# A shared expert begun inside the attention before it, value products one slot later, and gathers that add

## The chip, the cores and the metric

The kernel runs on one core of one Trainium2 chip. The metric is the time of one execution on the device in microseconds; the median of three runs of the kernel before is 1149.08 us (1148.59 to 1153.42). The engines have queues of their own and work in order: TensorE (PE, with its weight loads as PEld), VectorE (DVE), ScalarE (ACT), GpSimd (POOL) and SyncE (SP), which here only issues DMAs. They wait for one another on semaphores.

## The reference

All is in float32. x has 8 batches of 256 rows of 256 numbers. Eight layers follow one another, each added to x and each fed by the layer norm of x; the four attentions and experts among them are what the change touches:

```python
x = x + L0_xattn(norm(x), ctx, ...)     # attention 0: 16 heads, 77 context rows a batch, key mask, bias
x = x + L0_ffn(norm(x), ...)            # r * (relu(xk Wk)^2 Wv) with a token shift
x = x + L1_xattn(norm(x), ...)          # gelu MLP
x = x + L1_ffn(norm(x), ...)            # 8 experts, the best 2 for each row, width 352
x = x + L2_xattn(norm(x), ctx, ...)     # attention 2, causal mask
x = x + L2_ffn(norm(x), ...)            # shared expert, width 512, plus the best 1 of 8 experts
x = x + L3_xattn(norm(x), ctx, ...)     # attention 3
x = x + L3_ffn(norm(x), ...)            # int8 linear layer with one scale for all rows
```

`L2_ffn` is the shared expert `silu(x @ wg.T) * (x @ wu.T) @ wd.T` for all rows, and beside it for each row the expert with the largest logit of `x @ gate_w.T`, fed with the row times the logistic function of that logit.

## The kernel before

x stays in the core's memory (`X`, 16 tiles of 128 rows). The stages run one after another: setup, a0 (attention 0), f (both middle layers), e1 (the routed experts, 39 tiles of rows sorted by expert), a2 (attention 2), s2 (the shared expert, 16 tiles), e2 (its routed experts, 23 tiles), a3 (attention 3), q3. Each stage ends with `end_stage` (L334 to L337): PE, DVE, ACT and POOL drain, count up one semaphore, and wait until all four have.

An attention goes over 32 units, four to a batch. Its code is a loop over slots, written alike in the program of each engine; in a slot an engine does a step for several units at different stages of progress. The small functions at L255 to L291 say in which slot each step of batch b stands: the output projection in slot 4b + 7, the residual add in 4b + 8, the deviations of the next norm in 4b + 9, the transposes of its rows in 4b + 10, the logits of the router (a2 alone) in 4b + 11. For unit u, PE makes the scores in slot u (L1515), DVE adds the bias to them (L1020, L1024) and takes the maximum (L1028), POOL subtracts it (L584), ACT takes the exponential (L775), DVE sums and inverts (L1036, L1038), POOL or ACT copies the small parts (L569, L571 or L782, L784), PE transposes the probabilities (L1524 to L1526) in slot u + 2, ACT copies them out of PSUM (L798), and PE multiplies them with the values (L1538, L1541) in slot u + 3. Two units later DVE scales the product (L1047), PE projects a batch (L1447), DVE adds it to X (L955) and takes the statistics (L962, L967), POOL makes deviations and shifts (L518 to L529), ACT normalises (L734), and PE transposes the normalised rows (L1425).

In a2 and a3 the rows of the routed experts before must be put back into x first. POOL gathers them from DRAM with an indirect DMA (L549) into a buffer `YG`, two batches deep, and DVE adds them to X (`add_gathered`, L991 to L1006): in a2 with a gate for each row (L1002), in a3 plainly (L1005), two 128x256 adds a batch. Then come the statistics of the batch.

s2 is a `tile_pipeline` (L347 to L357): body s does one step for each of four successive tiles. On PE these are the gate and up products (L1731) of tile s - 1, the transposes of the product (L1741) of tile s - 2, and the down product (L1753) of tile s - 3. ACT copies the normalised transposed rows (L891), takes silu (L902), copies the transposes (L908); DVE multiplies (L1345) and adds to X (L1357). Beside that stands the routing for e2: DVE's `one_expert` (L1276), `tiles_of_experts` (L1287), `slots_of_rows` (L1303) in the first three bodies, PE's counts (L1700, L1701), and for each tile the normalised rows that DVE writes out (L1334) and POOL scatters to DRAM (L667). The weights of the down product come by a load that SP issues behind the border of a2 (L485, L487), and the last two experts' weights behind it (L491, L492).

Of the kernel before, what the change touches and what calls it, by code (L numbers as in the profile page):

```python
# [11 lines left out]
ALU = mybir.AluOpType  # L12
# [3 lines left out]
P = 128  # L16
B, S, D = 8, 256, 256
# [52 lines left out]
def build(nc, a):  # L70
    with ExitStack() as ctx:
# [58 lines left out]
        def carve(sizes, at=0):  # L130
            views = []
            for n in sizes:
# [75 lines left out]
        w_loaded = sem("w_loaded"); moe_loaded = sem("moe_loaded"); shared_loaded = sem("shared_loaded")  # L208
# [38 lines left out]
            ("setup", "a0", "f", "e1", "a2", "s2", "e2", "a3", "q3"))}  # L247
# [4 lines left out]
        LAYER = dict(a0=0, a2=1, a3=2)  # L252

# [46 lines left out]
        def slots_of(stage):  # L300

            return range(gather_slot(0, 0, 0, 1) if stage in FED_FROM else 0, transpose_slot(B - 1) + (2 if stage == "a2" else 1))
# [29 lines left out]
        FED = dict(a2=0, a3=B)  # L332
# [14 lines left out]
        def tile_pipeline(engine, body, tiles, depth):  # L347

            warm = -(-depth // 2) + 1
            for s in range(2 * warm):  # L350
                body((s, s % 2, s // 2), lambda lag, s=s: lag <= s)
# [43 lines left out]
        def _(sp):  # L395
# [116 lines left out]
        def _(pool):  # L512
# [27 lines left out]
            def gathers(stage, s):  # L540
# [3 lines left out]
                for b in range(B):  # L544
                    for t in range(T):
                        for k in range(K):
                            if gather_slot(b, t, k, K) == s:
                                after(pool, gathered_used, FED[stage] + b - 1 if b >= 2 else 0)
                                pool.indirect_dma_start(  # L549
                                    YG[stage][b % 2][:, t, k], None, BUFS[fed][1][:, :],  # L550
                                    bass.IndirectOffsetOnAxis(ap=slot_u[:, k, b * T + t:b * T + t + 1], axis=0)
                                ).then_inc(gathered[b % 2], 16)

            def attention(stage):
                layer, norms, order = LAYER[stage], NORM[stage], ORDER[stage]
                u0 = NU * layer
                for s in slots_of(stage):
# [18 lines left out]
                    bd = batch_at(deviations_slot, s)  # L576
# [8 lines left out]
                    bt = batch_at(transpose_slot, s)  # L585
# [1242 lines left out]
```

## Time and profile before

| what | us |
|---|---|
| median of three runs (lowest to highest) | 1149.08 (1148.59 to 1153.42) |
| the profiled execution | 1156.12 |
| its span | 1154.4 |
| PE busy | 917.6 (79%) |
| DVE busy | 570.6 (49%) |
| ACT busy | 445.6 (39%) |
| POOL busy | 382.6 (33%) |
| mean granted clock of PE, of full speed | 0.879 |

The shares are means over stages with different limits, so the profile is read by stretches: what each engine is busy with there, at which granted clock, and for what it waits. In a row of the timeline stand the start, the duration, the engine, the line of the kernel, the operation, what it writes and reads, how many instructions are taken together, and in brackets how long the engine was idle before and what ended that. Durations of matmuls overlap a little, so steps are taken from start to start.

### The profile page before, as it was taken

How to read it: one execution, taken by the hardware profiler on the slowest of the kernel's cores; microseconds unless marked ns; L12 is line 12 of the kernel's file. 1: busy time of each engine (PE TensorE's matmuls, PEld its weight loads, DVE VectorE, ACT ScalarE, POOL GpSimd, SP SyncE). 2: the span in 40 equal slices, each digit the busy share in tenths (PEclk: the TensorE clock that was granted, in tenths of full speed). 3: DMA queues.
4: the chain of work that ended last, by engine and by line, in shares of the span. 5: the costliest groups of instructions: out<-in, count | busy, mean ns of one | idle time of the engine just before them, and what ended most of it. 6: DMA issues, size and time to landing. Idle time of an engine off the chain costs nothing. (4 is left out here: it accounts for less than half of the span.)

```text
span 1154.4 us, 18959 instructions
## 1 busy us (share of the span) xinstructions
PE 917.6 (79%) x5718; PEld 625.3 (54%) x5719; DVE 570.6 (49%) x1298; ACT 445.6 (39%) x874; POOL 382.6 (33%) x725
## 2 busy tenths in 40 slices
PE   6688865887699999916767759996999996867773
PEld 5455544776466666614445535663666664545541
DVE  4688854675621222238776724221111135687764
ACT  4355534653132222215544532221222224546544
POOL 5556632355300000056664511110000024566540
PEclk9799987998599999957887969998999996888885
DMA  5599003011221111139000012002111110000002
GB/s 173 181 373 384 29 1 114 10 47 42 85 71 59 59 57 59 53 75 360 29 28 10 2 36 110 23 24 68 43 44 45 41 44 19 14 11 15 2 1 74
DMA packets 72861, 84.17 MB, mean 73 GB/s; under 512 B 8299, under 2 KB 64595, under 8 KB 72787
## 3 DMA queue, kind: packets, MB, share of 16 engines
q1 hardware_dynamic: 68179, 70.65, 18.5%
q0 software_dynamic: 4608, 12.59, 3.3%
q8 instruction: 40, 0.66, 0.2%
q14 instruction: 34, 0.28, 0.1%
HBM read 45.73 MB, written 37.49 MB: 72 GB/s over the span
## 5 line engine op out<-in xcount | busy, mean ns | idle before, releaser
L1731 PE MATMUL PS<-WE,tmp 128*128 x496 | 186.5, 520 | 0.0
L1345 DVE TENSOR_TENSOR tmp<-PS,tmp 128x352 f32<-128x352 f32 (+1 forms) x78 | 47.4, 608 | 270.9 <-ACT tmp L902 270.7
L584 POOL TENSOR_TENSOR tmp<-tmp,small 128x616 f32<-128x616 f32 x96 | 116.6, 1215 | 114.5 <-DVE small L1028 113.9
L798 ACT ACTIVATE tmp<-PS 128x768 f32<-128x768 f32 x96 | 78.0, 812 | 140.2 <-PE PS L1526 139.7
L902 ACT ACTIVATE tmp<-PS 128x352 f32<-128x352 f32 (+1 forms) x78 | 41.5, 532 | 221.4 <-PE PS L1731 221.4
L1731 PEld LDWEIGHTS PS<-WE,tmp 128*128 128x128 f32 x496 | 91.6, 195 | 60.2 <-issue 35.8
L1753 PE MATMUL PS<-WE,tmp 128*128 (+1 forms) x418 | 101.0, 380 | 2.1 <-DVE tmp L1361 2.1
L1524 PE MATMUL PS<-ident,tmp 128*128 128x128 f32 x384 | 70.3, 313 | 39.2 <-POOL rsx L571 24.8
L549 POOL DMA_INDIRECT WE<-ys,slot_u x32 | 32.2, 1005 | 196.6 <-DMA ys<-tmp 187.9
L1425 PE MATMUL PS<-ident,XN 128*128 128x128 f32 x208 | 40.8, 329 | 62.2 <-ACT XN L734 61.9
L734 ACT ACTIVATE XN<-X,SHIFTS,RSTDS 128x256 f32<-128x256 f32 x104 | 56.6, 594 | 83.3 <-POOL SHIFTS L529 83.2
L1524 PEld LDWEIGHTS PS<-ident,tmp 128*128 128x128 f32 x384 | 50.5, 159 | 58.9 <-POOL rsx L571 34.0
L1028 DVE TENSOR_REDUCE small<-tmp 128x8 f32<-128x616 f32 x96 | 76.3, 795 | 8.9
L1753 PEld LDWEIGHTS PS<-WE,tmp 128*128 128x128 f32 (+1 forms) x418 | 74.6, 190 | 10.9 <-issue 3.3
L1036 DVE TENSOR_REDUCE small<-tmp 128x8 f32<-128x616 f32 x96 | 75.0, 782 | 4.4 <-issue 3.2
L1538 PE MATMUL PS<-tmp,VL 32*32 32x128 f32 x768 | 43.5, 299 | 40.4 <-ACT tmp L798 35.8
L775 ACT ACTIVATE tmp<-tmp 128x616 f32<-128x616 f32 x96 | 68.5, 713 | 17.3 <-POOL tmp L584 16.8
L1425 PEld LDWEIGHTS PS<-ident,XN 128*128 128x128 f32 x208 | 27.2, 165 | 78.0 <-issue 59.8
L1447 PE MATMUL PS<-W,tmp 128*128 128x256 f32 x256 | 67.2, 409 | 1.6 <-ACT XT L741 1.6
L1731 PE MATMUL PS<-W,tmp 128*128 128x512 f32 x128 | 60.0, 613 | 4.4 <-DMA tmp<-in_L_sdT 4.4
L894 ACT ACTIVATE tmp<-PS 128x256 f32<-128x256 f32 x62 | 23.9, 385 | 89.4 <-PE PS L1719 89.4
L1024 DVE TENSOR_TENSOR tmp<-PS,tmp 128x616 f32<-128x616 f32 x64 | 50.2, 784 | 16.3 <-PE PS L1515 16.0
(251 smaller groups left out, 1678.9 us busy)
## 6 DMA issues: line engine op xcount, KB each, us to landing
xs_regions<-WE SPq DMA_DIRECT2D x11, 1536.0 KB, 13.7
ys<-tmp SPq DMA_DIRECT2D x62, 128.0 KB, 1.7
WE<-in_L_w SPq DMA_DIRECT2D x16, 352.0 KB
tmp<-xs_regions SPq DMA_DIRECT2D x39, 128.0 KB, 2.0
WE<-in_L_rgT SPq DMA_DIRECT2D x8, 512.0 KB
WE<-in_L_ruT SPq DMA_DIRECT2D x8, 512.0 KB
WE<-in_L_rdT SPq DMA_DIRECT2D x8, 512.0 KB
tmp<-xs SPq DMA_DIRECT2D x23, 128.0 KB, 2.0
```

The lines of the kernel that those rows point to most:

```text
L584: pool.tensor_tensor(sc, sc, spread(mx[:, q], SK), ALU.add).then_inc(shifted, 1)
L734: last = act.activation(dst[:, t], X[:, row], ACT.Identity, scale=RSTDS[:, row:row + 1], bias=SHIFTS[:, row:row + 1])
L775: act.activation(SC[:, k % 4], SC[:, k % 4], ACT.Exp, scale=FAR if stage == "a3" else 1.0).then_inc(exp_done, 1)
L798: act.activation(PT[:, u % 4], PT_PSUM, ACT.Copy).then_inc(pt_ready, 1)
L1024: dve.tensor_tensor(sc.rearrange("p (c h k) -> p c h k", c=CHUNKS, k=SK), S_PSUM.rearrange("p c (h k) -> p c h k", k=SK), bias, ALU.add).t ...
L1028: dve.tensor_reduce(mx[:, k % 2], sc.rearrange("p (h k) -> p h k", h=HG), AX.X, ALU.max, negate=True).then_inc(max_ready, 1)
L1036: dve.tensor_reduce(sm[:, q], SC[:, k % 4].rearrange("p (h k) -> p h k", k=SK), AX.X, ALU.add)
L1425: last = pe.transpose(PS[:, BANK_X, g * S + t * P:g * S + (t + 1) * P], src[:, t, g * P:(g + 1) * P], ident[:, :])
L1447: last = pe.matmul(PS[:, bank, t * D:(t + 1) * D], left[:, c, t * P:(t + 1) * P], right[:, c], start=c == 0, stop=c == G - 1)
L1524: pe.transpose(PT_PSUM[:, c * P:(c + 1) * P], p[:, c * PAIR:c * PAIR + P], ident[:, :])
L1731: last = pe.matmul(PS[:, 2 * q + k, 0:F], XS[:, q, c], w, start=c == 0, stop=c == G - 1)
L1753: last = pe.matmul(PS[:, 6, 0:D], HT[0:n, q, c], w, start=c == 0, stop=c == chunks - 1)
```

## The change

Three things change.

- There is no border between a2 and s2. The first four bodies of the shared expert's pipeline stand in the last slots of a2, on PE, ACT and DVE, and the pipeline goes on from body 4. On PE the gates of tile 0 stand behind the last transposes of probabilities, those of tile 1 with the transposes of tile 0 behind the last output projection, those of tile 2 with the transposes of tile 1 and the down product of tile 0 behind the last transposes of rows. The routing moves: `one_expert` to the end of a2, the counts and `tiles_of_experts` to body 4, `slots_of_rows` and the first four rows out to body 5. Since tiles 0 and 1 have by then been added to X, POOL keeps a copy of their rows, from which the first two rows out are made. SP's load of the down weights waits for the last output projection, with a semaphore of its own.
- In a0 the value products and all that follows them stand one slot later (`LATE`).
- In a3 the indirect DMA adds the gathered rows to X itself; DVE's adds, the buffer and the wait for its release are gone.

The diff, cut to its core:

```diff
-        YG = dict(a2=(WE[:, (E - 1) * EW:(E - 1) * EW + 2 * T * D], QTf[:, 0:2 * T * D]),
-                  a3=(WE[:, EW:EW + T * D], WE[:, EW + T * D:EW + 2 * T * D]))
-        YG = {stage: [f.rearrange("p (t k d) -> p t k d", t=T, d=D) for f in pair] for stage, pair in YG.items()}
+        YG = [f.rearrange("p (t k d) -> p t k d", t=T, d=D)
+              for f in (WE[:, (E - 1) * EW:(E - 1) * EW + 2 * T * D], QTf[:, 0:2 * T * D])]
...
+        LATE = dict(a0=1, a2=0, a3=0)
...
+        def first_tile(body, s):
+
+            body((s, s % 2, s // 2), lambda lag: lag <= s)
+
+        def tile_pipeline(engine, body, tiles, depth, begun=0):
+
+            warm = 3 if begun else -(-depth // 2) + 1
+            for s in range(begun, 2 * warm):
+                first_tile(body, s)
...
-            sp.wait_ge(stage_done, 4 * ST["a2"])
-
+            sp.wait_ge(o_psum, SUM["a2"] + B)
             sp.dma_start(shared_wd.rearrange("p (c d) -> p c d", c=4),
-                         a["L2_sdT"].rearrange("(c p) d -> p c d", p=P)).then_inc(shared_loaded, 16)
+                         a["L2_sdT"].rearrange("(c p) d -> p c d", p=P)).then_inc(down_loaded, 16)
...
-                                after(pool, gathered_used, FED[stage] + b - 1 if b >= 2 else 0)
-                                pool.indirect_dma_start(
-                                    YG[stage][b % 2][:, t, k], None, BUFS[fed][1][:, :],
-                                    bass.IndirectOffsetOnAxis(ap=slot_u[:, k, b * T + t:b * T + t + 1], axis=0)
-                                ).then_inc(gathered[b % 2], 16)
+                                rows_of = bass.IndirectOffsetOnAxis(ap=slot_u[:, k, b * T + t:b * T + t + 1], axis=0)
+                                if stage == "a3":
+                                    pool.indirect_dma_start(X[:, b * T + t], None, BUFS[fed][1][:, :], rows_of,
+                                                            compute_op=ALU.add).then_inc(gathered[b % 2], 16)
+                                    continue
+                                after(pool, gathered_used, b - 1 if b >= 2 else 0)
+                                pool.indirect_dma_start(YG[b % 2][:, t, k], None, BUFS[fed][1][:, :],
+                                                        rows_of).then_inc(gathered[b % 2], 16)
...
-                    bd = batch_at(deviations_slot, s)
+                    bd = batch_at(deviations_slot, s - LATE[stage])
...
-            end_stage(pool, "a2")
+            pool.wait_ge(ot_ready, NU)
+            pool.tensor_copy(XD[:, 2:4], X[:, 0:2]).then_inc(raw_kept, 1)
...
+                    if stage == "a2" and s == NU:
+                        act.wait_ge(s_taken, u0 + NU)
+                        first_tile(shared_tile, 0)
+                    if stage == "a2" and s in (NU + 2, NU + 5, NU + 6):
+                        first_tile(shared_tile, {NU + 2: 1, NU + 5: 2, NU + 6: 3}[s])
+
+                if stage != "a2":
+                    end_stage(act, stage)
...
+                if stage == "a3":
+                    return
                 for k in range(K):
                     if k:
                         dve.drain()
                     for t in range(T):
-                        x, y = X[:, b * T + t], YG[stage][b % 2][:, t, k]
-                        if stage == "a2":
-                            last = dve.scalar_tensor_tensor(out=x, in0=y, scalar=gate[:, k, b * T + t:b * T + t + 1], in1=x,
-                                                            op0=ALU.mult, op1=ALU.add)
-                        else:
-                            last = dve.tensor_tensor(x, x, y, ALU.add)
+                        x = X[:, b * T + t]
+                        last = dve.scalar_tensor_tensor(out=x, in0=YG[b % 2][:, t, k],
+                                                        scalar=gate[:, k, b * T + t:b * T + t + 1], in1=x,
+                                                        op0=ALU.mult, op1=ALU.add)
                 last.then_inc(gathered_used, 1)
...
-                    if s % 2 == 0 and 4 <= s <= NU + 2:
-                        scaled_outputs((s - 4) // 2)
+                    if bl is not None and stage == "a2" and s < NU:
+                        logits_copied_from(bl)
+                    if (s - LATE[stage]) % 2 == 0 and 4 <= s - LATE[stage] <= NU + 2:
+                        scaled_outputs((s - LATE[stage] - 4) // 2)
...
+                    if stage == "a2" and s == NU + 3:
+                        first_tile(shared_tile, 1)
+                    if stage == "a2" and s == NU + 4:
+                        logits_copied_from(B - 2)
+                        first_tile(shared_tile, 2)
+                    if stage == "a2" and s == NU + 7:
+                        first_tile(shared_tile, 3)
+                        logits_copied_from(B - 1)
+                        one_expert()
+                dve.drain()
+                if stage != "a2":
+                    end_stage(dve, stage)
...
-                    if stage == "s2" and isinstance(i[0], int) and i[0] < 3:
-                        (one_expert, tiles_of_experts, slots_of_rows)[i[0]]()
-                    if stage == "s2" and live(2):
+                    if stage == "s2" and isinstance(i[0], int):
+                        if i[0] == 4:
+                            tiles_of_experts()
+                        if i[0] == 5:
+                            slots_of_rows()
+                            for t in range(2):
+                                rows_out_of_x(t, 2 + t, 0, XD[:, 2 + t])
+                            for t in (2, 3):
+                                rows_out_of_x(t, t % 2, 0)
+                        if i[0] == 3:
+                            dve.wait_ge(raw_kept, 1)
+                    if stage == "s2" and (not isinstance(i[0], int) or i[0] >= 6) and live(2):
                         rows_out_of_x(i[0] - 2, i[1], (i[2] - 1) * 16)
...
+                    if 0 <= s - 3 - LATE[stage] < NU:
+                        values(s - 3 - LATE[stage])
...
-                    bo = batch_at(out_proj_slot, s)
+                    bo = batch_at(out_proj_slot, s - LATE[stage])
...
+                    if stage == "a2" and s == NU + 1:
+                        pe.wait_ge(s_taken, u0 + NU)
+                        pe.wait_ge(shared_loaded, 16 * 2)
+                        first_tile(shared_tile, 1)
+                    if stage == "a2" and s == NU + 3:
+                        pe.wait_ge(pt_ready, u0 + NU)
+                        first_tile(shared_tile, 2)
+                        next_logits(B - 2)
+                    if stage == "a2" and s == NU + 6:
+                        pe.wait_ge(down_loaded, 16)
+                        first_tile(shared_tile, 3)
+
+                if stage != "a2":
+                    end_stage(pe, stage)
```

PE's row at the end of a2, before: from the last value products on (L1538, L1541; L1425 transposes rows, L1491 makes logits, L1447 is the output projection, L1731 the gates of a tile, L1700 and L1701 the counts, L1741 its transposes).

```order
L1538 MATMUL PS<-tmp,VL 32x128 x4
L1541 MATMUL PS<-tmp,WE 32x128 x4
L1425 MATMUL PS<-ident,XN 128x128 x4
L1491 MATMUL PS<-WR,XT 128x8 x4
L1447 MATMUL PS<-WE,tmp 128x256 x4
L1425 MATMUL PS<-ident,XN 128x128 x4
L1491 MATMUL PS<-WR,XT 128x8 x4
L1731 MATMUL PS<-W,tmp 128x512 x4
L1700 MATMUL PS<-tmp 128x128
L1701 MATMUL PS<-tmp 128x128
L1731 MATMUL PS<-W,tmp 128x512 x4
L1741 MATMUL PS<-ident,tmp 128x128 x4
```

The same stretch of PE after the change, from the gates of tile 0 on (L1792 gates, L1802 transposes of a tile, L1814 down product; L1586 and L1589 value products, L1473 rows, L1495 output projection, L1539 logits).

```order
L1792 MATMUL PS<-W,tmp 128x512 x4
L1586 MATMUL PS<-tmp,VL 32x128 x4
L1589 MATMUL PS<-tmp,WE 32x128 x4
L1473 MATMUL PS<-ident,XN 128x128 x4
L1495 MATMUL PS<-WE,tmp 128x256 x4
L1792 MATMUL PS<-W,tmp 128x512 x4
L1802 MATMUL PS<-ident,tmp 128x128 x4
L1539 MATMUL PS<-WR,XT 128x8 x4
L1473 MATMUL PS<-ident,XN 128x128 x4
L1792 MATMUL PS<-W,tmp 128x512 x4
L1802 MATMUL PS<-ident,tmp 128x128 x4
L1814 MATMUL PS<-tmp 128x256 x4
```

Three gates, two transposes of tiles and one down product now stand among the attention's last steps, ahead of the last logits; the counts have moved behind the gates of tile 3.

DVE's row in a steady batch of a3, before, with what it waits for (L1005 adds the gathered rows, L962 and L967 are the statistics).

```order
L1020 SCALAR_TENSOR_TENSOR tmp<-PS,tmp 128x616 [waits s_copied,s_psum]
L1028 TENSOR_REDUCE small<-tmp 128x8 [waits shifted]
L1005 TENSOR_TENSOR X<-X,WE 128x256 [waits gathered0]
L1005 TENSOR_TENSOR X<-X,WE 128x256
L962 BN_STATS st<-X 128x6 x2
L967 BN_AGGR mv<-st 128x2 [waits veps_ready]
L967 BN_AGGR mv<-st 128x2
L1036 TENSOR_REDUCE small<-tmp 128x8 [waits exp_done]
```

The same place after the change (L980 and L985 are the statistics, L1046 the maximum, L1065 the scaled outputs, L1101 the maximum for q3).

```order
L1038 SCALAR_TENSOR_TENSOR tmp<-PS,tmp 128x616 [waits s_copied,pt_psum,s_psum]
L1046 TENSOR_REDUCE small<-tmp 128x8 [waits shifted]
L1065 TENSOR_TENSOR tmp<-PS,tmp 128x256 [waits pv_done]
L980 BN_STATS st<-X 128x6 [waits gathered0]
L980 BN_STATS st<-X 128x6
L985 BN_AGGR mv<-st 128x2 [waits veps_ready]
L985 BN_AGGR mv<-st 128x2
L1101 TENSOR_REDUCE amax<-XN 128x1 [waits xn_ready]
L1054 TENSOR_REDUCE small<-tmp 128x8 [waits pt_psum,exp_done]
```

The two adds are gone; the wait for the gather is now on the first of the statistics.

## Rows read from the trace of the kernel before

**Rows 1.** Windows: stretch; its length and PE, PEld, DVE, ACT, POOL busy; clock; DMA.
```profile
650.00:670.00 20.00, 13.44 (x159) 8.82 (x157) 13.85 (x30) 10.99 (x24) 8.87 (x15) 0.99 0.00 1
669.15:697.18 28.03, 15.79 (x55) 10.10 (x55) 4.44 (x16) 6.32 (x11) 2.04 (x8) 0.51 0.28 102
697.18:708.02 10.84, 10.84 (x40) 6.17 (x38) 7.67 (x37) 3.69 (x8) 0.00 (x0) 1.00 0.22 77
700.00:780.00 80.00, 80.00 (x286) 48.51 (x286) 25.72 (x74) 20.27 (x43) 13.52 (x14) 1.00 0.07 23
50.00:150.00 100.00, 83.51 (x941) 56.46 (x941) 81.03 (x154) 53.12 (x84) 61.81 (x120) 0.97 0.73 255
```

**Rows 2.** Timeline of PE at the border of attention 2 and the shared expert.
```profile
668.88 0.27 PE L1526 MATMUL PS<-ident,rsx 128*128 128x128 f32 x1
...
675.32 3.75 PE L1447 MATMUL PS<-WE,tmp 128*128 128x256 f32 x8 [0.36 <-DVE LG L1064]
...
684.11 1.09 PE L1425 MATMUL PS<-ident,XN 128*128 128x128 f32 x4 [5.03 <-ACT XN L734]
...
692.21 6.05 PE L1731 MATMUL PS<-W,tmp 128*128 128x512 f32 x8 [4.39 <-DMA tmp<-in_L_sdT]
...
702.42 3.60 PE L1731 MATMUL PS<-W,tmp 128*128 128x512 f32 x8
705.85 0.60 PE L1741 MATMUL PS<-ident,tmp 128*128 128x128 f32 x4
706.29 1.89 PE L1753 MATMUL PS<-tmp 128*128 128x256 f32 x8
708.02 3.60 PE L1731 MATMUL PS<-W,tmp 128*128 128x512 f32 x8
```

**Rows 3.** Timeline of DVE, and of SP's queue, at the same border.
```profile
679.18 0.69 DVE L955 TENSOR_TENSOR X<-X,PS 128x512 f32<-128x512 f32 x1 [4.01 <-PE PS L1447]
...
703.71 0.16 DVE L1305 COPY tmp<-tmp 128x8 f32<-128x8 f32 x1
...
707.57 0.41 DVE L1334 TENSOR_SCALAR tmp<-X,MEANS,RSTDS 128x256 f32<-128x256 f32 x1
...
707.89 0.69 DVE L1345 TENSOR_TENSOR tmp<-PS,tmp 128x512 f32<-128x512 f32 x1
...
708.99 0.42 DVE L1357 TENSOR_TENSOR X<-X,PS 128x256 f32<-128x256 f32 x1
...
688.16 0.37 SPq L487 DMA_DIRECT2D tmp<-in_L_sdT  x1
```

**Rows 4.** Timeline of PE, then of DVE, in a batch of attention 0.
```profile
95.40 0.54 PE L1515 MATMUL PS<-KBD,tmp 32*128 32x154 f32 x8
96.38 0.42 PE L1538 MATMUL PS<-tmp,VL 32*32 32x128 f32 x8 [0.43 <-ACT tmp L798]
...
109.91 0.54 PE L1515 MATMUL PS<-KBD,tmp 32*128 32x154 f32 x8
...
99.18 0.69 DVE L955 TENSOR_TENSOR X<-X,PS 128x512 f32<-128x512 f32 x1 [1.48 <-PE PS L1447]
```

**Rows 5.** Attention 3: line L1005, a batch's timeline (DVE, POOL, PE), line L549.
```profile
L1005 DVE TENSOR_TENSOR X<-X,WE x16: 412/1154/1495, 945.6 to 1072.2; 128x256 f32<-128x256 f32 x16
...
1030.22 2.57 DVE L1005 TENSOR_TENSOR X<-X,WE 128x256 f32<-128x256 f32 x2
...
1031.06 1.45 POOL L588 TENSOR_TENSOR X<-X,rows 128x512 f32<-128x512 f32 x1
...
1034.12 0.18 POOL L518 COPY MEANS<-mv 128x2 f32<-128x2 f32 x1 [1.61 <-DVE mv L967]
...
1036.18 0.66 PE L1524 MATMUL PS<-ident,tmp 128*128 128x128 f32 x4 [3.21 <-POOL rsx L571]
...
L549 POOL DMA_INDIRECT WE<-ys,slot_u x16: 944/1035/1039, 937.7 to 1059.0; - x16
...
DMA to landing us min/median/max: 2.7/2.8/3.1
```

More of the change, by code:

```diff
@@ L300, in slots_of @@
         def slots_of(stage):
-            return range(gather_slot(0, 0, 0, 1) if stage in FED_FROM else 0, transpose_slot(B - 1) + (2 if stage == "a2" else 1))
+            return range(gather_slot(0, 0, 0, 1) if stage in FED_FROM else 0, transpose_slot(B - 1) + LATE[stage] + (2 if stage == "a2" else 1))
         def norm_order(stage):
@@ L790, in attention @@
                         xt_evacuate_at(norms + order["in", bi], bi)
[L791 removed]
+                    bt = batch_at(transpose_slot, s - LATE[stage])
                     if bt is not None:
@@ L877, in _, with expert_tile @@
             end_stage(act, "f")
-            def experts(stage):
+            def expert_tile(stage):
                 F, u0 = WIDTH[stage], FIRST[stage]
@@ L894, in body @@
                             act.activation(XS[:, q], PS[:, 7, 0:D].rearrange("p (g s) -> p g s", g=G), ACT.Copy).then_inc(xs_ready, 1)
-                    if stage == "s2" and isinstance(i[0], int) and i[0] == 1:
-                        act.wait_ge(route_dve, 1)
-                        act.activation(score[:, :], top[:, 0], ACT.Tanh, scale=0.5).then_inc(route_act, 1)
                     if live(1):
@@ L912, in body, with experts @@
                         last.then_inc(ht_ready, 1)
-                tile_pipeline(act, body, NT if stage == "s2" else SLOTS[stage], 2)
+                    if stage == "s2" and isinstance(i[0], int) and i[0] == 4:
+                        act.wait_ge(route_dve, 1)
+                        act.activation(score[:, :], top[:, 0], ACT.Tanh, scale=0.5).then_inc(route_act, 1)
+                return body
+            def experts(stage, body, begun=0):
+                tile_pipeline(act, body, NT if stage == "s2" else SLOTS[stage], 2, begun)
                 end_stage(act, stage)
-            experts("e1")
+            shared_tile = expert_tile("s2")
+            experts("e1", expert_tile("e1"))
             attention("a2")
-            experts("s2")
-            experts("e2")
+            experts("s2", shared_tile, 4)
+            experts("e2", expert_tile("e2"))
             keys_evacuate(G, False)
@@ L1362, in body, with experts @@
                             dve.drain().then_inc(y_ready, 1)
-                tile_pipeline(dve, body, NT if stage == "s2" else SLOTS[stage], 3)
+                return body
+            def experts(stage, body, begun=0):
+                tile_pipeline(dve, body, NT if stage == "s2" else SLOTS[stage], 3, begun)
                 end_stage(dve, stage)
+            shared_tile = expert_tile("s2")
             slots_of_results()
@@ L1565, in attention @@
                     bl = batch_at(logits_slot, s)
-                    if bl is not None and stage == "a2":
+                    if bl is not None and stage == "a2" and s != NU + 3:
                         next_logits(bl)
@@ L1574, in attention @@
                         queries(bq)
-                    bo = batch_at(out_proj_slot, s)
+                    bo = batch_at(out_proj_slot, s - LATE[stage])
                     if bo is not None:
                         out_projection(bo)
-                    for slot_of, which in ((in_transpose_slot, "in"), (transpose_slot, "out")):
-                        bt = batch_at(slot_of, s)
+                    for slot_of, which, late in ((in_transpose_slot, "in", 0), (transpose_slot, "out", LATE[stage])):
+                        bt = batch_at(slot_of, s - late)
                         if bt is not None and (which, bt) in order:
@@ L1732, in body @@
                         last.then_inc(h_psum, 1)
-                    if stage == "s2" and isinstance(i[0], int) and i[0] == 1:
+                    if stage == "s2" and isinstance(i[0], int) and i[0] == 4:
                         counts()
@@ L1754, in body, with experts @@
                         last.then_inc(y_psum, 1)
-                if stage == "s2":
-                    pe.wait_ge(shared_loaded, 16 * 3)
-                else:
+                return body
+            def experts(stage, body, begun=0):
+                if stage != "s2":
                     pe.wait_ge(moe_loaded, MOE_LOADED[stage])
-                tile_pipeline(pe, body, NT if stage == "s2" else SLOTS[stage], 3)
+                tile_pipeline(pe, body, NT if stage == "s2" else SLOTS[stage], 3, begun)
                 end_stage(pe, stage)
+            shared_tile = expert_tile("s2")
             pe.wait_ge(blocks_ready, 8)
-            experts("e1")
+            experts("e1", expert_tile("e1"))
             pe.wait_ge(w_loaded, 16 * 7)
             attention("a2")
-            experts("s2")
-            experts("e2")
+            experts("s2", shared_tile, 4)
+            experts("e2", expert_tile("e2"))
             pe.wait_ge(w_loaded, 16 * 11)
```

47 lines of the change are left out of this document (18 added, 29 removed).

## Prediction

> **What bounds the kernel now.** The windows by stretch come first, since every stage has another limit. In attention 0 no engine is full: in the hundred microseconds from 50 PE works 83.51 and DVE 81.03 [rows 1]. In the shared expert PE has no gap, 80.00 of 80.00 at full clock [rows 1]; nothing beside it costs time there unless it stops PE. Between them lies the end of attention 2: from 669.15, the end of the last transposes, to 697.18 PE works 15.79 of 28.03 us, with a granted clock of 0.51, which is the lower level, 1.2 GHz, nearly throughout; before it the clock was 0.99 [rows 1]. Then the timeline of PE at that border: the output projection of the last batch takes 3.75 us, the normalised rows are waited for 5.03, and after the last logits the first gate matmuls start at 692.21 behind 4.39 us of waiting for the shared down weights, whose load is issued only at 688.16, past the border [rows 2, 3]. They run at the lower level for 6.05 us; the next take 3.60 [rows 2]. Last, the waits of a steady batch in attentions 0 and 3, below.
>
> **The border.** What the change removes is a stretch of PE. Both kernels do the same work between the end of the last transposes and the gates of tile 3 (708.02 before): 38.87 us. In units of the full clock the work in it is 15.79 x 0.51 + 10.84 = 18.9 [rows 1]. After the change PE has a tile's gates to do whenever it waited: gates 0 cover the wait for the last copied probabilities, gates 1, transposes and a batch's logits the 5.03 us for the normalised rows (3.43 + 0.44 us and the logits), gates 2 the copy behind them. The down weights are asked for when the last projection is done (679.07 before, about 678 after); they took 692.21 - 688.16 = 4.05, so they are there at 682.5, and gates 2, which wait for them, come at about 685: hidden with 2 us to spare.
>
> The clock falls before gates 0 have begun to count, so I charge them their measured 6.05 against 3.60: 2.45; and 1 us for waits of under half a microsecond that stay. 18.9 + 2.45 + 1 = 22.3, against 38.87: 16.5 saved [rows 1, 2]. One cost comes back: route work that stood beside the slow first gates now stands in bodies 4 to 6. Body 5 of DVE holds the slot numbers (703.71 to 707.57, 3.86), four rows out at 0.41, a product at 0.69 and an add at 0.42: 6.6 us against a tile of PE of 5.6: gates 3.43, transposes 0.44, down 1.73, from start to start between 702.42 and 708.02 [rows 2, 3]. The difference and some waits, 1.0 to 1.5 us, show once as a PE wait for the output buffer to be read. **Border: -15.** Bounds: if the clock stays low until gates 3, the 18.9 become 38, and hardly 1 us is saved; if the low clock and the route work cost nothing, 38.87 - 18.9 - 1 = 19. I take -15 since dense gates brought the clock back at 697.18, five microseconds after their start [rows 1, 2].
> The copy of the raw rows on POOL and the early table load of ACT lie in stretches in which those engines waited; POOL worked 2.04 us of the 28.03 [rows 1]. The six expert loads go out about 10 us sooner behind the shared load, off the path.
>
> **Attention 0, values one slot later.** Scores of two successive batches start at 95.40 and 109.91: 14.5 us a batch. In each of four slots PE waits 0.43 for the copied probabilities before its value product, and DVE waits 1.48 once a batch for the output projection before the residual add [rows 4]. One slot later both are there. Then DVE needs 14.5 - 1.48 = 13.0 and PE 14.5 - 4 x 0.43 = 12.8: DVE is the bound. Ends: nothing (if the loop turns on POOL's shift and DVE's maximum), and 7 x 1.48 = -10.4. New: queries stand one slot behind the projection and wait for its buffer to be read, a few tenths. I take 13.35 a batch, nearest the DVE figure: seven intervals of 1.15, **-8**. The tail has one slot more, but its value products were waiting there for the copies, so it costs nothing.
>
> **Attention 3, adding gathers.** DVE's pair of adds takes 2.57 in a steady batch; one alone took 0.41 at the least and 1.15 at the median [rows 5]. Behind it come the statistics, then POOL's deviations (1034.12, after a wait of 1.61 for DVE), then the copies that PE waits 3.21 for [rows 5]. When the adds go, the statistics are ready before POOL has finished its bias add (1031.06 + 1.45 = 1032.5), so that is late next: POOL starts at 1032.5 instead of 1034.12, 1.6 a batch. Six batches have the pair on the chain; of two of them I take 1.5, between twice 0.41 and 2.57: 4 x 1.6 + 2 x 1.5 = 9.4. The first batches, before POOL is busy, give 2 x 0.41 = 0.8: -10. Against it stands the issue on POOL. A gather's issue takes 1.04 there, and two stand in each batch just ahead of the copies that PE waits for [rows 5]. What an adding one takes no row shows. Below: as long as the plain one, and if it was issued without its wait a little less: -11. Above: if it doubles, 13 issues on the chain by 1.04 cost 13, so the stage loses 3. I take a quarter of a microsecond more each, near the row: -10 + 3, **-7**. Landing (2.7 to 3.1) is covered by some 15 us between issue and use; only at the stage's start is it open, once [rows 5].
> The trace shows only the issue of plain gathers, at 1.04. The Trainium skill, in "Collectives: The Full Stack", section "The bandwidth ceiling: the fold count and why AG ≠ RS ≠ AR", says that an add on the way needs two source reads and so two read descriptors a chunk where a copy needs one. If POOL's time goes by descriptors, the sum would be rival C's 1129; by the row alone the gathers cost 3 less than I take, 1116. No run here shows it yet.
>
> **Sum.** -15 - 8 - 7 = -30 on the profiled execution's own 1156.12 (its span is 1154.4): 1126.1. That execution is 7 us above the median of the runs, 1149.08; in proportion, 1149.08 x 1126.1 / 1156.12 = 1119.
>
> **Rivals.** A: the clock does not come back in the tail, because short transposes and waits lie between the gates. For it: from 669.15 to 697.18 it stayed low through 3.75 us of projection [rows 1, 2]. Against: those stood beside idle times of 5.03 and 4.39. If it comes back only with the end of gates 1, two gates (6.9), the projection (half of 3.75) and some 1.3 of values and transposes run at the low level and lose their own 10.1 again, of which 2.45 are charged: 7.6 more, border -8, total -23, 1126. [...]
> B: attention 0 turns on DVE-POOL-ACT hand-overs, not on the waits that go; PE and DVE both had about a fifth idle [rows 1]. Then 0 there: -22, 1127.
> C: the adding gather's issue doubles: stage +3, total -20, 1129.
> D, the slower side: an adding gather holds POOL for several microseconds. POOL works in order, so each slot's copies and PE's transposes queue behind; 13 on the chain. With -10 for the adds and -23 elsewhere it decides from 33 / 13 = 2.5 us extra an issue. At 4 extra: -33 + 52 = +19, 1168. Against it: nothing in the row of 1.04 hints at such a size.
> E: the change does less than it says everywhere (A, B and C together): -8 + 0 + 3 = -5, 1144.
>
> **Chances.** Forecast 0.57, with its own range of 1111 to 1125 (border -19 to -13, attention 0 -10 to -6, attention 3 -11 to -4: -37 to -23, rounded out); A 0.13, B 0.13, C 0.09, D 0.04, E 0.04. A measurement of this kernel tells 0.5%, 5.7 us, from no change. The forecast, A, B, C are faster: 0.92; E lies at that bound and is put to the same: 0.04; D is slower: 0.04. Range: down to 1109 for the low end with 2 us of spread between runs; up past A, B and C, and two of them together (A and C: 1136): 1137.
>
> **What would show it.** PE's timeline after: gates directly behind the last transposes, no wait on the down weights, 22 to 23 us from there to the gates of tile 3, the clock back at 1.0 before gates 1 end. A wait of PE on DVE at body 6 of about 1 us. Scores in attention 0 about 13.3 apart, no wait of DVE at the residual add, PE's 0.43 gone. In attention 3 no DVE adds, POOL's deviations directly behind its bias add, batches 1 to 2 us shorter, the gather's issue at 1.0 to 1.3. I am wrong if the border's clock is low past gates 1, if batches of attention 0 stay at 14.5, or if the gathers' issue row exceeds 2 us.

## The result, and the profile after

The changed kernel took 1120.37 us in the median of four runs (1118.30 to 1122.87), the kernel before on the same chip 1149.30; the ratio is 0.9742, with an interval of 0.9712 to 0.9772. In the first set of experiments it was 1119.39 against 1152.47, ratio 0.9711 (0.9686 to 0.9736). The profiled execution took 1122.87, with a span of 1121.0.

Windows of the changed kernel at the border and in attention 0 (columns as in [rows 1]):

```profile
662.18:667.00 4.82, 4.82 (x18) 1.87 (x18) 0.00 (x0) 1.79 (x3) 0.00 (x0) 0.81 0.00 0
662.18:683.29 21.11, 19.34 (x90) 11.58 (x89) 4.69 (x11) 9.11 (x17) 2.51 (x9) 0.96 0.50 175
50.00:150.00 100.00, 85.80 (x975) 59.19 (x973) 85.80 (x162) 56.32 (x90) 65.96 (x125) 0.96 0.73 256
```

From the end of the last transposes of probabilities (the gates of tile 0 follow them at 662.18) to the gates of tile 3 (683.29) it is 21.11 us, of which PE works 19.34 at a granted clock of 0.96. Before, the same stretch took 38.87, with PE's clock at 0.51 for the first 28.03 of it [rows 1]. In attention 0 PE and DVE both work 85.80 of a hundred microseconds, where they worked 83.51 and 81.03.

PE's timeline at the border after the change:

```profile
662.18 4.54 PE L1792 MATMUL PS<-W,tmp 128*128 128x512 f32 x8
...
668.89 1.97 PE L1495 MATMUL PS<-WE,tmp 128*128 128x256 f32 x8 [0.88 <-ACT XT L747]
...
670.69 3.60 PE L1792 MATMUL PS<-W,tmp 128*128 128x512 f32 x8
...
676.41 0.63 PE L1473 MATMUL PS<-ident,XN 128*128 128x128 f32 x4 [0.89 <-ACT XN L740]
676.88 3.60 PE L1792 MATMUL PS<-W,tmp 128*128 128x512 f32 x8
...
683.29 3.68 PE L1792 MATMUL PS<-W,tmp 128*128 128x512 f32 x8
...
700.18 1.97 PE L1814 MATMUL PS<-tmp 128*128 128x256 f32 x8 [1.13 <-DVE X L1399]
```

The gates of tile 0 take 4.54 us: the clock is at its lower level when they start, and back within them (0.81 in the mean of that stretch, and the projection behind them 1.97 where it took 3.75 [rows 2]). The 5.03 us for the normalised rows are now 0.89, since gates 1, transposes and logits stand ahead of them. No wait on the down weights is left. Last row: in body 6 PE waits 1.13 for DVE's add.

DVE and SP's queue there:

```profile
698.79 0.73 DVE L1366 TENSOR_SCALAR tmp<-X,MEANS,RSTDS 128x256 f32<-128x256 f32 x2
...
699.61 0.42 DVE L1399 TENSOR_TENSOR X<-X,PS 128x256 f32<-128x256 f32 x1
...
670.89 0.37 SPq L489 DMA_DIRECT2D tmp<-in_L_sdT  x1
```

The add (L1399) comes behind the slot numbers and four rows out. The down weights are asked for at 670.89, right when the last projection is done, and gates 2, which need them there, start at 676.88 without a wait for them.

A batch of attention 0 (PE, then DVE):

```profile
95.81 0.63 PE L1473 MATMUL PS<-ident,XN 128*128 128x128 f32 x4 [0.79 <-ACT XN L740]
...
97.02 0.54 PE L1563 MATMUL PS<-KBD,tmp 32*128 32x154 f32 x8
...
98.20 1.99 PE L1495 MATMUL PS<-W,tmp 128*128 128x256 f32 x8
...
106.68 0.65 PE L1572 MATMUL PS<-ident,tmp 128*128 128x128 f32 x4 [0.89 <-POOL rsx L576]
...
110.73 0.54 PE L1563 MATMUL PS<-KBD,tmp 32*128 32x154 f32 x8
...
100.30 0.69 DVE L973 TENSOR_TENSOR X<-X,PS 128x512 f32<-128x512 f32 x1 [0.71 <-PE PS L1495]
```

Scores of successive batches are 110.73 - 97.02 = 13.71 apart instead of 14.51 [rows 4]. PE's waits for copied probabilities are gone. In their place stand 0.79 for normalised rows and 0.89 for POOL's copy, and DVE still waits 0.71 for the projection (1.48 before).

Attention 3 (the gather's line, then DVE, POOL and PE in one batch):

```profile
L552 POOL DMA_INDIRECT X<-ys,slot_u x16: 1534/1610/1622, 914.7 to 1024.6; - x16
...
1010.79 0.75 DVE L980 BATCH_NORM_STATS2 st<-X 128x6 f32<-128x256 f32 x2
...
1016.02 1.61 POOL L552 DMA_INDIRECT X<-ys,slot_u  x1 [0.17 <-issue]
1017.07 0.86 POOL L574 COPY LB<-tmp 128x104 f32<-128x104 f32 x1
1017.29 0.87 POOL L576 COPY rsx<-small 128x128 f32<-128x128 f32 x1
...
1019.71 1.26 POOL L593 TENSOR_TENSOR X<-X,rows 128x512 f32<-128x512 f32 x1
1020.92 0.19 POOL L520 COPY MEANS<-mv 128x2 f32<-128x2 f32 x1
...
1018.21 0.66 PE L1572 MATMUL PS<-ident,tmp 128*128 128x128 f32 x4 [1.38 <-POOL rsx L576]
...
1021.15 3.78 PE L1495 MATMUL PS<-W,tmp 128*128 128x256 f32 x8
```

An adding gather holds POOL for 1.60 us against 1.04 for a plain one [rows 5], and the copies behind it (L574, L576) run slowed until it is over. POOL's deviations (1020.92) follow its bias add directly, without the wait of 1.61. PE still waits 1.38 at 1018.21 for the copies behind the second gather of the batch, where it waited 3.21 [rows 5], and the projection behind that wait runs at the lower level (3.78).

The adding gathers also move in other pieces. The DMA queue that carries POOL's transfers (packets, MB, share of the time of 16 DMA engines), before and after:

```profile
q0 software_dynamic: 4608, 12.59, 3.3%
```

```profile
q0 software_dynamic: 6144, 12.59, 4.1%
```

The bytes are the same (12.59 MB), but there are 1536 packets more, 96 for each of the 16 adding gathers. With the overwriting gathers of an experiment below it is 4608 again.

Marks in the two profiles give the share of each part. First scores to last residual add in attention 0: 127.35 before, 121.78 after, 5.6 less. Last transposes of attention 2 to the first gather of attention 3: 268.8 to 252.7, 16.1 less. That gather to attention 3's last residual add: 186.4 to 176.35, 10.1 less. The spans differ by 33.4; what remains, 1.6, lies in stages with the same code in both. Each of these is the difference of two single executions; the traces of the experiments show by how much a stage differs with the same code.

### The profile page after: what moved, and what is told of

Its sections match the earlier page's. It is cut to its first block and busy times, and to the rows that moved or that the text cites. A ratio compares the mean times of both kernels' runs of the same rounds, so it can differ in the third digit from the quotient of the medians.

```text
span 1121.0 us, 18932 instructions
## 1 busy us (share of the span) xinstructions
PE 904.6 (81%) x5718; PEld 618.7 (55%) x5719; DVE 555.4 (50%) x1282; ACT 444.8 (40%) x874; POOL 391.8 (35%) x726
## 3 DMA queue, kind: packets, MB, share of 16 engines
q0 software_dynamic: 6144, 12.59, 4.1%
## 5 line engine op out<-in xcount | busy, mean ns | idle before, releaser
L1792 PE MATMUL PS<-WE,tmp 128*128 x496 | 186.5, 520 | 0.0
L1792 PEld LDWEIGHTS PS<-WE,tmp 128*128 128x128 f32 x496 | 91.6, 194 | 60.2 <-issue 35.9
L1814 PE MATMUL PS<-WE,tmp 128*128 (+1 forms) x418 | 101.0, 380 | 2.1 <-DVE tmp L1403 2.1
L1572 PE MATMUL PS<-ident,tmp 128*128 128x128 f32 x384 | 66.3, 299 | 37.7 <-POOL rsx L576 23.6
L1473 PE MATMUL PS<-ident,XN 128*128 128x128 f32 x208 | 38.2, 313 | 63.6 <-ACT XN L740 63.5
L556 POOL DMA_INDIRECT WE<-ys,slot_u x16 | 15.8, 988 | 190.8 <-DMA ys<-tmp 187.7
L1046 DVE TENSOR_REDUCE small<-tmp 128x8 f32<-128x616 f32 x96 | 76.3, 795 | 9.2 <-issue 0.5
L1814 PEld LDWEIGHTS PS<-WE,tmp 128*128 128x128 f32 (+1 forms) x418 | 74.6, 190 | 10.9 <-issue 3.3
L1572 PEld LDWEIGHTS PS<-ident,tmp 128*128 128x128 f32 x384 | 47.9, 152 | 55.8 <-POOL rsx L576 28.2
L1495 PE MATMUL PS<-W,tmp 128*128 128x256 f32 x256 | 74.4, 442 | 1.6 <-ACT XT L747 1.6
L1473 PEld LDWEIGHTS PS<-ident,XN 128*128 128x128 f32 x208 | 25.5, 157 | 78.0 <-issue 59.5
L1586 PE MATMUL PS<-tmp,VL 32*32 32x128 f32 x768 | 43.3, 298 | 25.6 <-ACT tmp L804 20.2
L1495 PEld LDWEIGHTS PS<-W,tmp 128*128 128x128 f32 x256 | 54.0, 221 | 13.6 <-issue 5.7
L1792 PE MATMUL PS<-W,tmp 128*128 128x512 f32 x128 | 58.6, 601 | 0.0
```

The source lines that it names most:

```text
L1046: dve.tensor_reduce(mx[:, k % 2], sc.rearrange("p (h k) -> p h k", h=HG), AX.X, ALU.max, negate=True).then_inc(max_ready, 1)
L1473: last = pe.transpose(PS[:, BANK_X, g * S + t * P:g * S + (t + 1) * P], src[:, t, g * P:(g + 1) * P], ident[:, :])
L1495: last = pe.matmul(PS[:, bank, t * D:(t + 1) * D], left[:, c, t * P:(t + 1) * P], right[:, c], start=c == 0, stop=c == G - 1)
L1572: pe.transpose(PT_PSUM[:, c * P:(c + 1) * P], p[:, c * PAIR:c * PAIR + P], ident[:, :])
L1792: last = pe.matmul(PS[:, 2 * q + k, 0:F], XS[:, q, c], w, start=c == 0, stop=c == G - 1)
L1814: last = pe.matmul(PS[:, 6, 0:D], HT[0:n, q, c], w, start=c == 0, stop=c == chunks - 1)
```

## The experiments

**The parts one by one.** The changed kernel once more, with the border alone changed, without the later slot in attention 0, and with plain gathers in attention 3. The edits are those of the diff, undone.

```diff
-        LATE = dict(a0=1, a2=0, a3=0)
+        LATE = dict(a0=0, a2=0, a3=0)
...
-                                    pool.indirect_dma_start(X[:, b * T + t], None, BUFS[fed][1][:, :], rows_of,
-                                                            compute_op=ALU.add).then_inc(gathered[b % 2], 16)
...
+                            last = dve.tensor_tensor(x, x, y, ALU.add)
```

The experiments were run in three sets, each beside the kernel before (medians 1152.47, 1152.59 and 1153.43), while the changed kernel ran in the first alone. Differences from the changed kernel in the later ones go across sets, and those of 1 or 2 us are not clear of that.

> The changed kernel once more, as the foot of the three runs beside it. Both theories: 29 us under the kernel before (1120), ratio 0.974.

> The border alone is changed; attention 0 and attention 3 are as before. Theory (three gains that add, as the marks of the two traces have them: border 16, attention 0 5 to 6, attention 3 10): 14 to 17 us under the kernel before, 1132 to 1135. Rival (the border gives nearly all, and what the traces show in the attentions is the profiled execution of before, which was 7 us over its median): 22 to 28 under it, 1121 to 1127.

> The changed kernel, but attention 0 with value products, projection, residual and rows in their old slots. Theory: 5 to 6 us over the changed kernel (1125 to 1126), batches of attention 0 again 14.5 us apart. Rival (the slot later is worth nothing in the median): within 1 us of the changed kernel.

> The changed kernel, but attention 3 with plain gathers and the 16 adds on DVE. Theory: 8 to 10 us over the changed kernel (1128 to 1130). Rival (gain of the adds eaten by the longer issue, 1.60 against 1.04): 0 to 3 over it.

| kernel | median us | ratio to before (interval) |
|---|---|---|
| before | 1152.47 | |
| changed | 1119.39 | 0.9711 (0.9686 to 0.9736) |
| border alone | 1135.83 | 0.9869 (0.9844 to 0.9894) |
| changed, attention 0 as before | 1128.07 | 0.9795 (0.9773 to 0.9817) |
| changed, plain gathers | 1132.26 | 0.9838 (0.9815 to 0.9861) |

The border alone is worth 16.6 us in the medians, as the theory of three parts had it; the rival, that it gives nearly all, falls. The two others came out larger than expected: taking the later slot away costs 8.7, the adding gathers 12.9, but both together only 16.4. In the traces the later slot shows as 3 to 6 us in attention 0: first scores to last residual add take 125.1 and 125.2 with it undone and 119.6 to 122.0 in seven profiles with it. The kernel before, with the old code there, took 127.35, so some 2 us of the 5.6 may be variation of that stage. Attention 3 from the first gather to the last residual add takes 172.8 to 176.4 in four profiles of kernels that have the same code there (the changed one twice, the one without the later slot, and the one without filling, below), and 183.1 to 186.4 in three with plain gathers and adds. So a stage varies by 2 to 4 us by itself. How much of the mismatch of 5.2 us (8.7 + 12.9 - 16.4) comes from that stays open.

**Is it the filling of the tail, or the barrier?** All three engines do their first shared bodies behind the last logits, without a border.

```diff
-                    if stage == "a2" and s == NU + 1:
-                        pe.wait_ge(s_taken, u0 + NU)
-                        pe.wait_ge(shared_loaded, 16 * 2)
-                        first_tile(shared_tile, 1)
...
+                if stage == "a2":
+                    pe.wait_ge(s_taken, u0 + NU)
+                    pe.wait_ge(shared_loaded, 16 * 2)
+                    pe.wait_ge(pt_ready, u0 + NU)
+                    first_tile(shared_tile, 1)
+                    first_tile(shared_tile, 2)
```

> The changed kernel without a border, but the first bodies of the shared expert stand behind the last logits on every engine, so nothing fills the attention's tail. Theory (the gain comes from PE's tail being filled, which also brings the clock back): 10 to 13 us over the changed kernel, 1130 to 1133, the clock low until some 5 us into the first gates. Rival (the gain is the barrier and the late load of the down weights): at most 4 over it.

Measured: 1132.97 (ratio 0.9835, 0.9807 to 0.9864), 13.6 over the changed kernel's median in the set before, both beside a kernel before of 1152.5. Windows and PE's timeline of this kernel:

```profile
660.40:679.06 18.66, 10.82 (x49) 7.84 (x49) 2.29 (x7) 5.90 (x10) 2.50 (x9) 0.50 0.42 142
679.06:684.00 4.94, 4.94 (x9) 2.16 (x10) 0.17 (x1) 0.07 (x1) 0.00 (x0) 0.63 0.56 206
...
666.72 3.75 PE L1489 MATMUL PS<-WE,tmp 128*128 128x256 f32 x8 [0.36 <-DVE LG L1071]
...
675.50 1.09 PE L1467 MATMUL PS<-ident,XN 128*128 128x128 f32 x4 [5.03 <-ACT XN L740]
...
679.06 8.93 PE L1783 MATMUL PS<-W,tmp 128*128 128x512 f32 x16
...
693.87 3.60 PE L1783 MATMUL PS<-W,tmp 128*128 128x512 f32 x8
```

The wait for the weights is gone here too, and the border still takes 693.87 - 660.40 = 33.5 us to the gates of tile 3. The projection takes 3.75 again, the rows are waited for 5.03 again, and the clock stays at 0.50 over the whole tail. So of the 17.8 us that the stretch lost, 5.4 are the barrier and the late load, and 12.4 are the filling, with the clock that it keeps; what the filled gaps and the clock give each by itself was not separated. The theory stands.

**What the longer issue costs.** The same gathers, but writing over X: the kernel leaves out the addition of the routed experts' rows.

```diff
-                                    pool.indirect_dma_start(X[:, b * T + t], None, BUFS[fed][1][:, :], rows_of,
-                                                            compute_op=ALU.add).then_inc(gathered[b % 2], 16)
+                                    pool.indirect_dma_start(X[:, b * T + t], None, BUFS[fed][1][:, :],
+                                                            rows_of).then_inc(gathered[b % 2], 16)
```

> The changed kernel, but the gathers of attention 3 write over X where they should add to it: the addition of the routed experts' rows to X is left out, the transfers and their place stay. Theory (the longer issue of an adding gather, 1.60 against 1.04, costs its difference about twice a batch): issue back at 1.0, attention 3 4 to 7 us shorter, total 1113 to 1116. Rival (POOL has room for the difference): within 1.5 us of the changed kernel.

Measured: 1114.01 (0.9658, 0.9633 to 0.9682), 5.4 under the changed kernel. The gather's line, the windows of four successive batches (residual add to residual add), and PE's wait behind the second gather of a batch:

```profile
L552 POOL DMA_INDIRECT X<-ys,slot_u x16: 946/1035/1038, 913.6 to 1019.9; - x16
...
963.83:981.33 17.50, 13.24 (x145) 8.70 (x144) 13.76 (x29) 11.56 (x19) 12.79 (x25) 1.00 0.06 16
981.33:1000.76 19.43, 16.21 (x146) 10.91 (x147) 13.84 (x30) 11.59 (x19) 14.21 (x27) 0.82 0.05 15
1000.76:1018.32 17.56, 13.12 (x145) 8.78 (x144) 13.76 (x28) 11.48 (x19) 11.42 (x24) 1.00 0.06 16
1018.32:1036.00 17.68, 13.11 (x145) 8.98 (x146) 13.75 (x29) 11.48 (x19) 11.67 (x24) 1.00 0.03 8
...
993.58 0.87 PE L1572 MATMUL PS<-ident,tmp 128*128 128x128 f32 x4 [0.82 <-POOL rsx L576]
```

The issue is back at its old size, and attention 3 takes 168.9 us from the first gather to the last residual add. PE waits 0.82 behind the gather instead of 1.38. The difference of 0.57 an issue on POOL goes with 5.4 us in all, which is ten times 0.57; but the windows don't show it standing on the chain ten times. Batches still come in two lengths with the same work. Those at a clock of 1.00 take 17.50 to 17.68, and the shorter ones of the changed kernel, at 0.97 and 0.98, 18.13 and 18.04 (below): about one difference of 0.57 a batch, though two issues stand in most of them. The rest of the steady part is the clock: one of these four batches is a long one (19.43 at 0.82), of the changed kernel's four two are. Whether the shorter issue keeps the clock up, or it fell less often by chance, stays open.

**Moving the issue.** The first gather of a batch between two copies, the second one slot later.

```diff
                         pool.tensor_copy(LB[:, q]..., left)
+                        if stage == "a3":
+                            gathers(stage, s, (0,))
                         pool.wait_ge(rsum_ready, u + 1)
                         pool.tensor_copy(rsx[:, q]..., spread(rs[:, q], DH)).then_inc(rsx_ready, 1)
+                        if stage == "a3":
+                            gathers(stage, s, (1,))
```

> The changed kernel, but POOL issues the adding gathers of attention 3 where it waited: the first of a batch between the two copies of a slot, the second one slot later ahead of its shift. Theory (the issue stands on the chain to PE's transposes): 4 to 8 us under the changed kernel, 1112 to 1116. Rival (POOL's work is the bound, wherever the issue stands): within 1.5 us of the changed kernel.

Measured: 1118.31 (0.9697, 0.9673 to 0.9720), within 1.1 of the changed kernel: the rival had the time. That POOL's work is the bound, its reason, is not shown: in the window below POOL works 65.14 of 90 us. A window of attention 3 in this kernel; then, in the changed one, the same stretch, four successive batches and PE's wait in the second of them:

```profile
950.00:1040.00 90.00, 68.79 (x715) 46.11 (x715) 66.68 (x135) 56.40 (x92) 65.14 (x119) 0.96 0.10 15
```

```profile
950.00:1040.00 90.00, 71.84 (x703) 47.95 (x697) 63.04 (x129) 55.44 (x92) 62.34 (x111) 0.88 0.10 14
967.58:987.23 19.65, 15.66 (x146) 10.55 (x145) 13.85 (x29) 11.48 (x19) 13.56 (x26) 0.85 0.11 15
987.23:1005.36 18.13, 13.67 (x145) 9.18 (x144) 13.76 (x29) 11.48 (x19) 12.45 (x24) 0.97 0.11 16
1005.36:1024.97 19.61, 15.94 (x146) 10.59 (x147) 13.83 (x29) 11.70 (x19) 15.55 (x27) 0.85 0.09 14
1024.97:1043.01 18.04, 13.46 (x145) 9.29 (x144) 13.76 (x29) 11.48 (x19) 10.79 (x23) 0.98 0.05 8
...
1000.52 0.66 PE L1572 MATMUL PS<-ident,tmp 128*128 128x128 f32 x4 [1.41 <-POOL rsx L576]
```

The clock is at 0.96 instead of 0.88, and the steady batches take 18.2 to 18.3, where the changed kernel has 18.04 and 18.13 at a clock of 0.98 and 0.97, and 19.61 and 19.65 at 0.85. So its longer batches are gone but its shorter ones don't get shorter; and a profile of the changed kernel came as low as 172.8 us over the stage, against 172.5 here.

**Issuing early.** Eleven of the sixteen gathers go out while PE makes keys and values and POOL has nothing to do; a semaphore for each batch.

```diff
+        EARLY_GATHERS = {-11: ((0, 0), (0, 1), (1, 0), (1, 1), (2, 0)), -5: ((2, 1), (3, 0), (3, 1)),
+                         -1: ((4, 0), (4, 1), (5, 0))}
...
+                    now = EARLY_GATHERS.get(s, ()) + tuple((b, t) for b in range(B) for t in range(T)
+                                                           if gather_slot(b, t, 0, 1) == s and (b, t) not in early)
```

> The changed kernel, but 11 of the 16 adding gathers of attention 3 are issued while PE still makes keys and values at the stage's start, where POOL waited; the last five stay in their slots; each batch has a semaphore of its own. Theory (an issue in a steady slot costs its 1.60 on the chain, as overwriting gathers at 1.04 gave 5 us): five issues fewer on the chain, 5 to 8 us under the changed kernel, 1111 to 1115. Rival (moving the issue moves nothing, as it was when two were moved by a slot): within 1.5 us.

Measured: 1114.30 (0.9663, 0.9641 to 0.9685), about 5 under the changed kernel and at the lower end of what the theory asked. Its gathers:

```profile
L555 POOL DMA_INDIRECT X<-ys,slot_u x16: 1537/1602/1790, 913.7 to 1020.4; - x16
...
DMA to landing us min/median/max: 3.6/3.8/4.6
```

They land 3.6 to 4.6 after the issue, where plain ones took 2.7 to 3.1 [rows 5]; DVE's statistics show no wait for a gather, here or in the changed kernel. This version beats both kernels. That five issues fewer on the chain are the cause is not shown: the one steady batch in which POOL issues none takes 17.48, but from the first gather to the last residual add attention 3 takes 171.4, against 172.8 and 176.4 in the two profiles of the changed kernel.

**What holds a batch of attention 0.** First the transposes of rows one slot later, then behind the transposes of probabilities, on top of early gathers.

```diff
-                    for slot_of, which, late in ((in_transpose_slot, "in", 0), (transpose_slot, "out", LATE[stage])):
+                    for slot_of, which, late in ((in_transpose_slot, "in", 0), (transpose_slot, "out", ROWS_LATE[stage])):
...
+                    if stage == "a0" and 2 <= s < NU + 2:
+                        transposes(s - 2)
```

> The changed kernel, but in attention 0 PE's transposes of the normalised rows and their copy stand one more slot later; PE waited 0.79 for them in each batch. Theory (that wait holds the batch at 13.7): batches 13.0 to 13.3, total 3 to 5 us under the changed kernel, 1115 to 1117. Rival (the batch is held by the hand-over from the projection to DVE and POOL): batches stay within 0.2 of 13.7, total within 1 us.

> The kernel with the rows of attention 0 one more slot later once more, for its trace, since the first had a disturbed profile. Its time moved nothing. Theory now: PE's wait of 0.79 for the normalised rows is gone, but the transposes now stand right behind the next projection and share its buffer in PSUM, so PE waits there for DVE's residual add, 0.7 to 1.2 a batch, and batches stay near 13.7. Rival: batches are 13.0 apart and the gain is lost in another stage.

> The kernel with early gathers, and in attention 0 PE's transposes of rows behind the transposes of probabilities of the same slot, so that PE does something while the normalised rows are made. Theory (batches of attention 0 are held by the projection that comes 0.79 late; DVE waits 0.71 for it): batches of 13.0 to 13.4, 2 to 5 us under the kernel with early gathers alone. Rival (the copy of the rows then delays ACT's copy of the probabilities and with it everything behind): within 1 us or slower.

Rows one slot later: 1121.93 in the first set (0.9724, 0.9695 to 0.9752), no gain: the first theory falls. In the trace, of an execution of 1125.86, PE, then DVE:

```profile
97.27 1.99 PE L1496 MATMUL PS<-W,tmp 128*128 128x256 f32 x8
100.16 0.63 PE L1474 MATMUL PS<-ident,XN 128*128 128x128 f32 x4 [0.90 <-issue]
...
99.37 0.69 DVE L974 TENSOR_TENSOR X<-X,PS 128x512 f32<-128x512 f32 x1 [0.58 <-PE PS L1496]
...
113.74 0.69 DVE L974 TENSOR_TENSOR X<-X,PS 128x512 f32<-128x512 f32 x1 [0.58 <-PE PS L1496]
```

The transposes of rows wait 0.90 behind the projection, until DVE has added it (99.37 + 0.69) and its buffer in PSUM, which the code gives to both, is free; the profile names no releaser here ("issue"). Residual adds are 113.74 - 99.37 = 14.37 apart: the wait was moved, and the batch became longer. The second theory on this kernel is borne out in the wait; its batch, near 13.7, is not.

Rows behind the transposes: 1116.84 (0.9693, 0.9667 to 0.9719), 2.5 over early gathers alone, and the two intervals overlap: no gain, as the rival had it. PE, then DVE:

```profile
96.27 0.65 PE L1583 MATMUL PS<-ident,tmp 128*128 128x128 f32 x4 [1.05 <-POOL rsx L584]
...
98.69 1.99 PE L1506 MATMUL PS<-W,tmp 128*128 128x256 f32 x8
...
100.79 0.69 DVE L981 TENSOR_TENSOR X<-X,PS 128x512 f32<-128x512 f32 x1 [0.98 <-PE PS L1506]
...
114.80 0.69 DVE L981 TENSOR_TENSOR X<-X,PS 128x512 f32<-128x512 f32 x1 [0.99 <-PE PS L1506]
```

The wait for the rows is gone, and PE waits 1.05 for POOL's copy instead; batches are 14.01 apart. DVE still waits 0.98 for the projection, more than the 0.71 of the changed kernel, so this edit did not make the projection come in time, and whether a timely one would shorten the batch was not tested. PE, POOL and DVE hand each unit around, and taking PE's wait away at one place moved it to another; which of these hand-overs sets 13.71 stays open.

## Why the prediction was right

The forecast was -30 us, 1119; it came to -28.9 in the first medians, 1120.4, to -33.1 in those of the first set of experiments, and to -33.25 between the two profiled executions (1156.12 and 1122.87).

- **Border, -15.** Measured -16.1 in the traces and -16.6 alone. Its steps held: 22.3 us from the transposes to gates 3, measured 21.1; gates 0 were charged 6.05 and took 4.54; the wait of PE in body 6, forecast at 1.0 to 1.5, is 1.13. Rival A, the clock that stays low, is what happens without the filling, as the experiment showed; with it the clock came back inside gates 0.
- **Attention 0, -8.** The direction was right and the size was off: 0.80 a batch instead of 1.15, 5.6 by the marks and 3 to 6 against kernels with the old code there. The term took it that DVE's wait of 1.48 goes whole and that DVE is then the bound. The wait fell to 0.71 only, and PE met two new waits (0.79 and 0.89); that these hold the projection back was not shown. The extra slot, put at nothing, cost something too: the first residual add comes 27.19 behind the first scores, where it came 25.94. Rival B, nothing at all, falls.
- **Attention 3, -7.** Measured -10.1, with both parts mis-sized. The extra issue was taken at 0.25 and is 0.57, which goes with 5 us in time (4 to 7 in the traces, the clock included) and not 3. The adds were taken at -10; with the adds left out and issues of the plain length attention 3 is 14 to 17 shorter (168.9 against 183.1 to 186.4). One thing that the term left out is PE's clock: in steady batches before it was 0.87 to 0.92, after it is 0.97 in some and 0.85 in others, and the latter are 1.5 us longer. That the clock makes that difference is read from the windows, and was not tested alone.
- Rival C (issue doubled, stage +3) had the right direction and came half way: 1.60 / 1.04 = 1.5, and the stage still gained. Rivals D and E fall. The Trainium skill's two read descriptors for an add ("Collectives: The Full Stack", "The bandwidth ceiling: the fold count and why AG ≠ RS ≠ AR") would have given 2 if POOL's time went by descriptors; the measurement, 1.5, decides. What the trace shows of the pieces is packets, 6144 instead of 4608 with the same bytes; that they set the issue's length is not shown.

The sum came out right partly by luck: a gain smaller than forecast in attention 0 (5.6 instead of 8) met a larger one in attention 3 (10.1 instead of 7). Its own range of 1111 to 1125 for the forecast should read 1112 to 1126 by its sums (-37 and -23).

## What to carry to other kernels

Where a stage ends in a chain of short steps on several engines, work of the next stage that doesn't depend on it paid twice here: it filled the gaps, and the clock was back 2 us after the first gates began. Removing the barrier alone gave less than a third of that stretch here. When an instruction moves onto a queue that sets the pace, price its issue there, and look first for a stretch in which that queue has nothing to do; and after a wait is removed, expect the next hand-over in the ring to take up part of the gain.

## What the runs showed that was not expected

In the changed kernel an adding gather holds POOL 1.53 to 1.62 us against 0.94 to 1.04 for one that overwrites at the same place, and small copies issued behind it take 0.86 instead of 0.27 until it is over. Batches of attention 3 with the same code came in two lengths within one execution, 18.1 and 19.6 us, the longer ones at a lower mean clock; in one of them a PE wait of 1.38 stands ahead of the stretch at the lower level. Such a wait is not enough by itself: in a batch of 18.13 PE waits 1.41 at the same place (1000.52), and the clock stays up behind it.
